# When VectorE rounds the feed-forward weight: tiles 2 to 33 or tiles 21 to 52 of the first stage

## The reference

```python
# layer 0
W = weights[itok_B_0_15]; c = einsum('bct,bcd->bdt', x, W)         # a 64x64 matrix for each batch item
probs = softmax(c @ W_router.T); top 2 of 8 experts, renormalised -> combine
h = einsum('nd,erd->ner', c, A) * combine
x = x + c @ W_base.T + b_base + 2.0 * einsum('ner,eor->no', h, B)
# layer 1
r = x @ base_weight.T + base_bias + (x @ A[id].T) @ B[id].T         # one of 32 adapters for each batch item
q = fp8(r * (1 / input_scale)); w_q = fp8(weight * (1 / weight_scale))
x = x + (q @ w_q) * (input_scale * weight_scale) + bias
```

## Time and profile before

| what | us |
|---|---|
| median of 3 runs | 2011.21 |
| the three runs | 2011.28, 2009.75, 2011.21 |
| the profiled execution, time | 2010.24 |
| the profiled execution, span | 2008.1 |

### The profile page before, as it was taken

The page is one execution under the profiler, slowest core; times in us unless marked ns, Lnnn a source line. Parts: engine busy times, 40 slices in busy tenths (PEclk is TensorE's granted clock), DMA queues, the critical chain, the costliest instruction groups (busy, mean ns, idle before and its releaser), DMA issues.

```text
span 2008.1 us, 38332 instructions
## 1 busy us (share of the span) xinstructions
PE 1973.0 (98%) x13056; PEld 1809.6 (90%) x13056; DVE 1437.2 (72%) x3881; ACT 400.1 (20%) x1083; POOL 494.7 (25%) x471
## 2 busy tenths in 40 slices
PE   6999999999999999999999999999999999999998
PEld 5998999999999999999988888888888888888887
DVE  6888878778766666666667766776677667766776
ACT  3111211212211111111121222122212221212121
POOL 2444343210110110110122222222222222222222
PEclk9999999999999999999999999999999999999999
DMA  6765444334334334333356655665566656665663
GB/s 208 211 207 149 125 144 145 104 118 125 104 104 120 96 96 127 97 96 118 105 158 175 160 162 149 175 159 162 149 173 160 161 150 170 161 161 152 169 163 108
DMA packets 220523, 290.07 MB, mean 144 GB/s; under 512 B 98102, under 2 KB 169784, under 8 KB 220476
## 3 DMA queue, kind: packets, MB, share of 16 engines
q1 hardware_dynamic: 220476, 289.57, 51.6%
HBM read 163.63 MB, written 109.06 MB: 136 GB/s over the span
## 4 chain that ended last, share of the span: by engine, by line
PE 91%; DVE 5%; issue 1%; DMA 1%; SPq 1%; ACT 1%; POOL 0%; DVEq 0%; ACTq 0%; POOLq 0%
PE bank_g L990 12%; PE bank_g L992 12%; PE bank_g L991 12%; PE bank_g L1051 12%; PE bank_g L1050 12%; PE bank_g L1049 12%; PE bank_y L1062 11%; PE bank_y L970 3%; PE bank_g L1095 1%; PE bank_g L1019 1%; PE bank_g L1017 1%; PE bank_g L1018 1%; DVE hwt L327 1%; DVE wq_pow L785 0%; DVE x_blocks L860 0%
## 5 line engine op out<-in xcount | busy, mean ns | idle before, releaser
L990 PE MATMUL bank_g<-w0h,st_h 128*128 128x384 f32 (+1 forms) x1536 | 526.0, 342 | 10.3 <-DVE ring L849 5.4
L992 PE MATMUL bank_g<-w0h,st_l 128*128 128x384 f32 (+1 forms) x1536 | 520.7, 339 | 0.0
L991 PE MATMUL bank_g<-w0l,st_h 128*128 128x384 f32 (+1 forms) x1536 | 520.7, 339 | 0.0
L1049 PE MATMUL bank_g<-w1h,st_h 128*128 128x352 f32 x1536 | 505.2, 329 | 0.5 <-ACT val L705 0.5
L1051 PE MATMUL bank_g<-w1h,st_l 128*128 128x352 f32 x1536 | 496.0, 323 | 0.0
L1050 PE MATMUL bank_g<-w1l,st_h 128*128 128x352 f32 x1536 | 495.1, 322 | 0.0
L990 PEld LDWEIGHTS bank_g<-w0h,st_h 128*128 128x128 f32 x1536 | 289.2, 188 | 27.6 <-issue 20.3
L771 DVE TENSOR_TENSOR st_l<-ring,st_h 128x512 fp32r<-128x512 f32 x128 | 142.3, 1112 | 228.5 <-ACT st_h L688 228.4
L1049 PEld LDWEIGHTS bank_g<-w1h,st_h 128*128 128x128 f32 x1536 | 288.6, 188 | 8.1 <-issue 0.8
L562 POOL TENSOR_TENSOR ring<-ring,b_base_sb 128x1024 f32<-128x1024 f32 x64 | 152.8, 2402 | 564.3 <-PE bank_y L970 534.3
L1050 PEld LDWEIGHTS bank_g<-w1l,st_h 128*128 128x128 f32 x1536 | 288.5, 188 | 1.6
(11 more groups left out here) (78 smaller groups left out, 1986.6 us busy)
## 6 DMA issues: line engine op xcount, KB each, us to landing
ring<-x SPq DMA_DIRECT2D x64, 512.0 KB, 3.9
x_scratch<-ring SPq DMA_DIRECT2D x64, 512.0 KB, 2.7
x1t_scratch<-x_blocks SPq DMA_DIRECT2D x256, 128.0 KB, 2.4
ring<-x1t_scratch SPq DMA_DIRECT2D x64, 512.0 KB, 3.6
ring<-x_scratch SPq DMA_DIRECT2D x64, 512.0 KB, 5.1
out<-obuf SPq DMA_DIRECT2D x64, 512.0 KB, 2.7
b_stack<-b_split SPq DMA_DIRECT2D x384, 64.0 KB, 3.7
raw<-a_split SPq DMA_DIRECT2D x128, 128.0 KB, 4.2
```

Source lines behind the costliest of these rows:

```text
L990: pe.matmul(to, st_h[:, rows], w0h[:, k, cols], start=(k == 0), stop=False)
L991: pe.matmul(to, st_h[:, rows], w0l[:, k, cols], start=False, stop=False)
L992: last = pe.matmul(to, st_l[:, rows], w0h[:, k, cols], start=False, stop=(k == KC - 1))
L1049: pe.matmul(to, st_h[:, rows], w1h_k[:, k, cols], start=(k == 0), stop=False)
```

## The change

Two numbers of the program change: the first tile with a piece of the feed-forward weight, 2 before and 21 after, and, for ScalarE, the tile at which its loop begins. By the first, pieces 0 to 31 come in tiles 21 to 52, `PREP_TILES` becomes 53 and `UNROLLED` 56, so four engines write out 56 tiles rather than 36 (34 for ScalarE). No operation is added or taken away. The loads of pieces 2 to 31 in the DMA queue move with them, from tiles 3 to 32 to tiles 22 to 51. GpSimd's splitting stays in tiles 0 to 20.

```diff
-WQ_FIRST_TILE = 2
+WQ_FIRST_TILE = 21
...
-                for t in range(PREP_TILES):
+                for t in range(UNROLLED):
                     tile(t, True)
                     if t == WQ_FIRST_TILE:
                         act.wait_ge(s_scale, 3)
                     if wq_piece(t) is not None:
                         scale_weight(wq_piece(t))
-                with act.Fori(PREP_TILES, TILES - 3, 2) as i:
+                with act.Fori(UNROLLED, TILES - 3, 2) as i:
                     tile(i, True)
                     tile(i + 1, True)
```

## The result

The changed kernel took 1997.24 us (median of 6, 1996.49 to 1997.73), the kernel before 2009.78 us (6 runs, 2007.70 to 2011.28). The ratio is 0.9936, with a 95% interval of 0.9925 to 0.9948, so the gain is 12.5 us, between 10.5 and 15.1. The forecast was 1999.8 us in a range of 1998.2 to 2004.5. The direction was right, the likeliest size 1.1 us short of this gain, and the time lies 1.0 us under the range. One execution of all, in the run with later splits, came out in a slower state (2161.6 us at a granted clock of 0.85) and is in none of the figures.

A forecast was written before the change was run, and what follows sets the result against it. TensorE, 91% of the chain, was taken as the bound, losing time to VectorE's lateness in tiles 3 to 12. 12.25 - 0.8 = 11.4 us off the median 2011.21 gave 1999.8 us, range 1998.2 to 2004.5.

The forecast's parts named there:

- Step 1: Pieces leave tiles 2 to 20, so L799 is no longer late in tiles 3, 5, 7, 8, 10: gain 12.25 us.
- Step 2: In tiles 4 to 8 L805 still stands behind GpSimd's bias add, forgiven: value 0, bounds 0 and 0.2 us each.
- Step 3: Casts in tile 10, now on time, have one or two of twelve caught: value 0, bounds 0 and 1 us.
- Step 4: In tile 9 L849 still waits for the bias queued behind the first w1 split: 0.8 us kept, bounds 0.6 and 1.0.
- Steps 5 to 7: Pieces entering tiles 35 to 52, their loads moving in the DMA queue, twenty tiles written out: no cost.
- The forgiven delay: VectorE lateness that TensorE absorbs, estimated at 0.6 to 1.0 us in odd tiles and 2.7 us in even ones.
- Rival C: Rounding lacks margin in tiles 35 to 52, bias adds right on it make the kernel slower, such as 2012.4 us; chance 0.03.
- A: The lock turns to the gate's own chain (L805, L808, L832, casts): gain only 4 to 9.5 us; chance 0.15.
- B: Lateness in tiles 3 to 10 comes from GpSimd's or the queue's order and stays: 2010 to 2012 us; chance 0.02.

The follow-up runs named there:

- six more: The changed kernel with L782's operation done six times more in each of the 32 pieces; 2083.71 us, ratio 1.0366.
- first adds wait: The run with w1 splits a tile later, with GpSimd's bias adds of tiles 0 and 1 waiting for their tile's hwt casts; 1997.29 us, ratio 0.9928.

## Why the prediction was short, step by step

**Step 1, the pieces leave: the mechanism right, the term mis-sized.** The pieces' overlap with the splits was the loss; moving either partner ends it, and the unrolling alone does nothing. The term was "12.25 us", read from one execution. Three executions with this overlap lost 12.25, 14.2 and 14.9 us (163.9, 165.9 and 166.6, less 151.65). The prediction had seen the fall of the clock in tile 10 and priced it at "some 1.7 us"; in the other two traces the clock stayed down for 6.8 us, 1.7 us more, and the casts of tile 11 were caught behind it. The step that failed is this term of the sum, which took the 12.25 us of one execution for the kernel's loss, and with it a range whose lower end was made of the other steps' bounds and of the spread of three runs. It gave this term no bound upwards. (Its two ends are not worked out alike: with half the spread, as at the upper end, the lower one would be 1998.75, farther still from the measured time.) The sum was then set against the median of three runs, 2011.21 us; six runs have 2009.78, so of the 2.6 us between forecast and measurement 1.1 are gain and 1.4 are this starting point.

**A term that was missing: the clock in the second stage.** The prediction took the second stage as equal in both. In the profiled pair it was 2.1 us of the difference, 1.7 of it by the clock. Of eleven traces without filling matmuls, of all kernels but the one with six more, four have the fall there (before, pieces from tile 12, one more AND, first adds wait), after waits of 2.3, 3.0, 2.0 and 2.6 us; seven have none, after waits of 1.8 to 2.9 us. So the length of the wait does not decide it. What does is left open.

**Step 2, L805 behind the bias add: right.** Timeline of tile 4 in the changed kernel:

```profile
90.39 2.40 POOL L562 TENSOR_TENSOR ring<-ring,b_base_sb 128x1024 f32<-128x1024 f32 x1
...
90.90 1.92 DVE L805 TENSOR_SCALAR probs<-expo,rsum 128x8 f32<-128x8 f32 x1
```

It stands 1.7 us and TensorE does not wait, as forecast.

**Step 3, the casts of tile 10: right.** All 120 casts of tiles 3 to 12 average 188 ns.

**Step 4, the wait in tile 9: right in kind, 0.6 for 0.8 us.** The timeline, against the earlier trace rows:

```profile
174.16 2.40 POOL L562 TENSOR_TENSOR ring<-ring,b_base_sb 128x1024 f32<-128x1024 f32 x1
...
176.60 0.42 DVE L849 TENSOR_TENSOR ring<-bank_g,ring 128x256 f32<-128x256 f32 x1 [1.11 <-POOL ring L562]
177.17 0.41 PE L990 MATMUL bank_g<-w0h,st_h 128*128 128x392 f32 x1 [0.38 <-DVE ring L849]
```

The run that moved the split by a tile took the 0.6 us away.

**Steps 5 to 7, no cost for tiles 35 to 52, the queue and the unrolling: right,** by L860's 469.2 us and by the run with the unrolling alone.

**The forgiven delay: wrong.** "I take 2.7 us" for an even tile counted only what TensorE can wait for. The bias adds of the next pair come first: once the 0.71 us of room are used up, two casts stand behind them, and the even tile loses 2.6 us, the pair 2.8 (43 us over 15 pairs). Nothing in the change reaches that edge, so the forecast did not suffer. Rival C, slower by bias adds in tiles 35 to 52, was placed at the rounding itself; its real place is the casts, and its distance was 0.7 us, not the several us that the prediction reasoned with.

**The rivals.** A did not come in the change, though its mechanism is real: it took part in tile 11 of the two traces with the longer fall of the clock, and it cost 4.6 us at the start of the run with later splits and 43 us in the one with two more ANDs. B is ruled out by moving either partner.

## What to carry to other kernels

Where VectorE and GpSimd both work, a short VectorE instruction can stand for a whole GpSimd instruction. Look at where GpSimd's long instructions lie beside the critical chain of VectorE, not at its busy share, and count the distance to the next one as the margin. A wait that orders the long one behind the chain is cheap insurance. A fall of TensorE's clock behind a wait makes a loss that differs between executions: here the same wait of 2.1 to 2.2 us was followed by 3.4 us at 1.2 GHz in one trace and by 6.8 us in two. So one trace gives a sample of it, and the range needs room on that side.

## What the runs showed that was not expected

A cliff: one added instruction of 0.3 us a tile cost nothing that can be told, a second one brought the cost to 43 us over 32 tiles. Behind one and the same wait in tile 10 the clock stayed down for 3.4 us in one trace and for 6.8 in two. The kernel before spread over 8.6 us in 49 runs (2005.89 to 2014.46), the changed one over 1.2 us in six. That the change made it steadier is not shown: the run with pieces from tile 12 and the one with one more AND, which lose nothing in tiles 2 to 12 either, each had an execution above 2002 us. Moving GpSimd's splits away let three bias adds run together and cost 4.6 us in the first tile. The clock fell after one and the same wait in some executions and not in others, at some 1.7 us each.
